# Two attention layers on one core: queries and keys contract 128 rows, the added ones zero

## The reference

```
q = einsum('oc,bcn->bon', Wq, xf) + bq[:, None]      # 32 rows
k = einsum('oc,bcn->bon', Wk, xf) + bk[:, None]      # 32 rows
v = einsum('oc,bcn->bon', Wv, xf) + bv[:, None]      # 256 rows
scores = einsum('bci,bcj->bij', q, k)
attn = softmax(scores, axis=1)
out = gamma * einsum('bcn,bnm->bcm', v, attn) + xf
```

```
energy = einsum('nid,ndj->nij', theta, phi)
attention = softmax(energy, axis=-1)
out = einsum('ncj,nij->nci', g, attention)
return gamma * conv1x1(out, out_w, out_b) + x
```

## Time and profile before

| | us |
|---|---|
| median of 3 runs | 2783.41 |
| lowest and highest | 2781.85, 2785.19 |
| the profiled execution | 2780.86 |
| its span, first to last instruction | 2779.1 |

### The profile page before, as it was taken

The page is one execution under the profiler, slowest core; times in us unless marked ns, Lnnn a source line. Parts: engine busy times, 40 slices in busy tenths (PEclk is TensorE's granted clock), DMA queues, the critical chain, the costliest instruction groups (busy, mean ns, idle before and its releaser), DMA issues.

```text
span 2779.1 us, 38409 instructions
## 1 busy us (share of the span) xinstructions
PE 2662.1 (96%) x11632; PEld 2092.5 (75%) x11632; DVE 2061.1 (74%) x3415; ACT 1743.6 (63%) x3171; POOL 1955.3 (70%) x1546
## 2 busy tenths in 40 slices
PE   7999999989999999998999999999899999999988
PEld 5777777777687777776678777777667777777756
DVE  7677777767777777776777777777676777777665
ACT  5566666667756666665765666666676566666557
POOL 3677777767867776775776776777577767777668
PEclk9999999999999999999999999999999999999989
DMA  2000000012100000001220000000121000000011
GB/s 87 1 16 16 19 21 19 21 39 69 62 31 23 16 23 16 16 16 39 70 76 24 19 21 16 16 16 16 46 77 61 16 16 16 16 16 16 16 46 62
DMA packets 45553, 85.23 MB, mean 31 GB/s; under 512 B 5032, under 2 KB 5160, under 8 KB 45352
## 3 DMA queue, kind: packets, MB, share of 16 engines
q1 hardware_dynamic: 37720, 68.41, 7.3%
q10 hardware_dynamic: 7632, 14.36, 1.7%
HBM read 48.96 MB, written 33.55 MB: 30 GB/s over the span
## 4 chain that ended last, share of the span: by engine, by line
PE 79%; DVE 11%; issue 5%; ACT 4%; POOL 1%; DMA 1%; SPq 0%; ACTq 0%; POOLq 0%; DVEq 0%
PE o_ps L908 17%; PE o_ps L911 17%; PE o_ps L912 16%; PE s_ps L885 9%; PE aux L948 8%; DVE mx L734 4%; DVE acc L696 3%; PE aux L922 2%; PE aux L986 1%; PE aux L969 1%; PE aux L965 1%; PE aux L926 1%; ACT queries L585 1%; DVE aux L775 1%; DVE osb L790 1%
## 5 line engine op out<-in xcount | busy, mean ns | idle before, releaser
L498 POOL TENSOR_TENSOR prob_l<-prob,prob_h 128x512 fp32r<-128x512 f32 x1280 | 1642.0, 1290 | 716.3 <-ACT prob_h L560 716.1
L557 ACT ACTIVATE prob<-s_ps 128x512 f32<-128x512 f32 x1280 | 766.1, 599 | 827.6 <-PE s_ps L885 824.0
L734 DVE TENSOR_REDUCE mx<-aux 128x1 f32<-128x512 f32 x1097 | 749.9, 684 | 309.1 <-PE aux L948 305.3
L908 PE MATMUL o_ps<-prob_h,vh 128*128 128x512 f32 x2304 | 926.8, 402 | 18.0 <-ACT osb L571 17.9
L911 PE MATMUL o_ps<-prob_l,vh 128*128 128x512 f32 x2304 | 914.4, 397 | 1.2 <-POOL prob_l L498 1.2
L912 PE MATMUL o_ps<-prob_h,vl 128*128 128x512 f32 x2304 | 904.7, 393 | 0.0
L696 DVE TENSOR_TENSOR acc<-prob,acc 128x512 f32<-128x512 f32 x1216 | 834.7, 686 | 76.7 <-ACT prob L557 61.8
L560 ACT ACTIVATE prob_h<-s_ps 128x512 fp32r<-128x512 f32 x1280 | 762.2, 595 | 0.0
L885 PE MATMUL s_ps<-queries,keys 98*128 98x512 f32 x1280 | 522.3, 409 | 22.7 <-DMA queries<-nm_turned 11.6
L908 PEld LDWEIGHTS o_ps<-prob_h,vh 128*128 128x128 f32 x2304 | 439.4, 191 | 129.9 <-ACT osb L571 29.2
L911 PEld LDWEIGHTS o_ps<-prob_l,vh 128*128 128x128 f32 x2304 | 438.7, 190 | 105.1 <-POOL prob_l L498 6.2
(11 more groups left out here) (131 smaller groups left out, 1886.0 us busy)
## 6 DMA issues: line engine op xcount, KB each, us to landing
xa<-x SPq DMA_DIRECT2D x32, 512.0 KB, 3.7
spill<-xa SPq DMA_DIRECT2D x32, 512.0 KB, 2.7
xa<-spill SPq DMA_DIRECT2D x32, 512.0 KB, 3.7
y<-xa SPq DMA_DIRECT2D x32, 512.0 KB, 2.8
xp<-x ACTq DMA_DIRECT2D x26, 512.0 KB, 3.7
queries<-nm_turned SPq DMA_DIRECT2D x236, 1.0 KB
xp<-x SPq DMA_DIRECT2D x2, 512.0 KB, 9.2
prob<-w_in ACTq DMA_DIRECT2D x1, 576.0 KB, 5.5
```

The lines of the kernel that those rows point to most:

```text
L498: nc.gpsimd.tensor_tensor(out=prob_l[:, i, :], in0=prob[:, i, :], in1=prob_h[:, i, :].bitcast(f32), op=ALU.subtract).then_inc(pl_ready, 1)
L557: nc.scalar.activation(prob[:, i, :], s_ps[s][:, :], ACT.Exp).then_inc(p_ready, 1)
L734: ins = nc.vector.tensor_reduce(out=dst, in_=bank[:, :], axis=AX.X, op=ALU.max)
L908: mm(o_ps[ct][:, :], value(vh, l, t, ct), prob_h[:, i, :], start=t == 0, stop=False)
```

## The change

All convolutions for keys and queries get weights of 128 columns, of which the last 32 are zero, and so write 128 rows; the bias of these rows is zero as well. ScalarE's copy of the queries to rows 64 to 95 covers rows 64 to 127 (`Q_PAD`), and so writes zeros into rows 96 to 127 of the chunk's queries; the maxima are written to rows 96 and 97 afterwards, as before. Rows 96 to 127 of `keys` are set to one at the start, in place of 96 and 97. The scores and the maxima's products contract all 128 rows: what is added is one times zero. The weights that are transferred and split are 1280 columns in place of 1152 (two parts of 640, before 576).

The order of the instructions on each engine, the waits and the plan stay as they are; only shapes change.

```
-WCOLS = 2 * R3 + C + DV
-W_KQ, W_V, W_G = (0, R3), 2 * R3, 2 * R3 + C
+WCOLS = 2 * P + C + DV
+W_KQ, W_V, W_G = (0, P), 2 * P, 2 * P + C
...
+        Q_PAD = slice(2 * DK, P)
...
-                    biased(l, q[KQ_Q, :], bank[KQ_Q, :], KQ_Q)
+                    biased(l, q[Q_PAD, :], bank[Q_PAD, :], Q_PAD)
...
-            nc.vector.memset(keys[0][NM, :].bitcast(f32), 1.0)
-            nc.vector.memset(keys[1][NM, :].bitcast(f32), 1.0)
+            nc.vector.memset(keys[0][R3:P, :].bitcast(f32), 1.0)
+            nc.vector.memset(keys[1][R3:P, :].bitcast(f32), 1.0)
...
-                mm(s_ps[h % SRING][:, :], keys[l][0:R3 + 2, t * P:(t + 1) * P], queries[0:R3 + 2, q_slot(l, b, n), :],
+                mm(s_ps[h % SRING][:, :], keys[l][:, t * P:(t + 1) * P], queries[:, q_slot(l, b, n), :],
                    start=True, stop=True).then_inc(s_full, 1)
...
-                    last = mm(dst[:, :], queries[0:R3, q_slot(l, b, c), sub * P:(sub + 1) * P],
-                              keys[l][0:R3, chunk(kc)], start=True, stop=True)
+                    last = mm(dst[:, :], queries[:, q_slot(l, b, c), sub * P:(sub + 1) * P],
+                              keys[l][:, chunk(kc)], start=True, stop=True)
...
-                    last = conv(dst[0:R3, :], W_KQ[l], R3, ROUND[Job("X", l, b, c, 0)])
+                    last = conv(dst[:, :], W_KQ[l], P, ROUND[Job("X", l, b, c, 0)])
...
+    def padded(rows):
+        return np.concatenate([rows, np.zeros((P - R3, C), np.float32)], axis=0)
-    w = np.concatenate([stacked(L0_conv_Wq, L0_conv_Wk, 0).T, stacked(L1_conv_phi_w, L1_conv_theta_w, 0).T,
+    w = np.concatenate([padded(stacked(L0_conv_Wq, L0_conv_Wk, 0)).T,
+                        padded(stacked(L1_conv_phi_w, L1_conv_theta_w, 0)).T,
                         np.asarray(L0_conv_Wv).T, np.asarray(L1_conv_g_w).T], axis=1)
```

## The result

The changed kernel takes 2745.14 us (median of 4 runs, 2742.38 to 2749.85), the kernel before 2782.63 beside it: a ratio of **0.9867, 95% interval 0.9848 to 0.9886**, 37 us less. Beside other kernels on a second occasion it took 2741.63 us against 2782.92, ratio 0.9856 (0.9841 to 0.9871). The forecast was 2737.5, 46 us less.

A forecast was written before the change was run, and what follows sets the result against it. TensorE's distances between product starts were taken to bound the kernel; -42.5 - 4 + 0.5 = -46 us took the profiled 2780.86 to 2735, and the median lying 2.5 above gave 2737.5 us, range 2724 to 2786.

The forecast's parts named there:

- What bounds the kernel: Whole span: TensorE's distance from one product's start to the next sets the time; TensorE works in 96% of the span.
- The floor and the steps: Attention steps: full products start 0.227 us apart; steps with one or two partial products fall to 1.59 and 1.82 us.
- Point 1: First layer's scores and maxima with 128 rows: 24 ns saved on each of about 1770 products, 11% left out, -42.5 us.
- Point 2: The same in the second layer: 330 products counted at half of 24 ns, -4 us, bounds 0 and -8.
- Points 3, 4 and 6: Convolutions' wider weight loads, ScalarE's wider copy of the queries with VectorE's fills, and unchanged queues: each forecast to cost nothing.
- Point 5: The start: weights of 1280 columns in place of 1152 take longer to prepare, +0.5 us, bounds 0.2 and 1.
- The clock: Around changes of layer: work that comes earlier may meet the half clock otherwise, 3 us each way.
- Rival A: Scores and maxima: their lone place between two groups costs, not their rows; no change, 2784 us; chance 0.26.
- Rival B: Scores and maxima: only the partial product's own distance shrinks, by 8 ns; 14 us less, 2770 us; chance 0.14.
- Rival C: Scores and maxima: a lone product with full rows is dearer, 5 ns more each; +9 us, 2793; chance 0.10.

## Why the prediction was right, and where it was off

- **What bounds the kernel**: right. TensorE's distances shrank and the time with them; the chain's shares are the same.
- **The floor and the steps**: right to the digit. 1.59 and 1.82 us were forecast, 1.587 and 1.813 measured. The steps with two maxima, which the forecast didn't look at, keep 13 to 18 ns of excess that has nothing to do with the row count.
- **Point 1, the size**: too large. 42.5 us over 32 chunks is 1.33 us a chunk, and 0.92 came. The step of the working that failed is the one price of 24 ns for every partial product, read from steps with one and two of them. Steps with three have 50 ns and not 72 (and 13 to 18 of the 50 are not the rows'), so the chunk held 1.2 us of excess to be won and not 1.5. And the share lost to waits, taken as 11%, was about a quarter, 0.3 of 1.2 us: beside VectorE's stretch, whose 0.19 us is what the 11% meant, there are the waits for the sums and the maxima's rows. Over the whole kernel the distances shrank by 42 us and 11 of these went into waits. That the 42 look like the forecast's 42.5 is chance: the forecast's figure is for the first layer alone and had the waits taken off.
- **Point 1, the reason**: right in its effect and wrong in its wording. Padding to 128 rows helps because everything around has 128 rows. 98 rows everywhere have the same distances.
- **Point 2, the second layer**: 4 us were forecast. From the first to the last product of attention its four stretches last 622.5 us together before, 620.7 in the first profile of the changed kernel and 613.8 in the second. The distances give 2.1 us in both, the waits take as much back (2.9 and 1.9), and what is left is the clock, 2.5 us in one and 8.3 in the other. So point 2 came to nothing, and the difference between the two profiles of one kernel is the clock.
- **Points 3, 4 and 6**, nothing: right, by the run with the padding alone. **Point 5**, half a microsecond, is too small to see; the interval of that run is 0.9988 to 1.0006.
- **The clock**, 3 us each way: too narrow, and not symmetrical. By the two levels the kernel before spends about 103 us at 1.2 GHz (a mean of 0.9815 over 2780 us), the changed one about 82 (0.985). If TensorE led in all of these 21 us, they are worth 10 us. Matched product by product the clock has 2.5 us of the gain in the first profile and 10.6 in the second, 8% and 25% of it, so it is not steady from run to run.
- **Rival A** had 0.26: out, by the runs with one odd product of attention and with 98 rows everywhere. The Trainium skill's rule that spoke for it, in "TensorE: Matmul & The Clock Gate", section "LDWEIGHTS (loading the stationary operand)", holds for the loads (189 to 191 ns for 96 to 128 rows), and says nothing of what a change of the count does to the products behind. **Rival B** is out, the whole echo went. **Rival C** is out: the distance after a full score is 0.227 us.

The errors partly cancel, and that is luck: 46 us were forecast from shorter distances net of waits, where about 31 came (42 less 11), and nothing from the clock, which gave 2.5 to 10.6.

## What to carry to other kernels

Where TensorE sets the time, read its product-to-product distances over twenty products and not the booked durations, and look for products whose number of contracted rows differs from their neighbours'. Give all of them the same number; zeros cost nothing here where rows had to be added, and one row short was as bad as thirty. An excess per item should be priced from every pattern in which the items stand, since it need not add up, and against the same pattern in the kernel after, since a part of it may have another cause. An engine that holds the chain for a while is not all that stands in the way: look at what the next one does in the same time.

## What the runs showed of the hardware that was not expected

- A change of the number of contracted rows between neighbouring products costs about 25 ns, spread over the next five products of 0.227 us. It comes both from 128 to 98 rows and back and is as large for 127 as for 98 rows. Two or three changes near one another cost 20 to 51 ns together and do not add up.
- The same row of longer distances stands behind a product that starts 5 ns late without any change of the row count, in the three-product steps of the changed kernel, where a weight load mostly starts 50 to 100 ns late. These steps are 13 to 18 ns above the floor on average.
- Changes of the bank, of the operands and of the loaded columns (96 or 128) cost nothing visible at that distance, nor do waits that are met before the weight load could start.
- The mean granted clock was lower with fewer rows in all the products: 0.976 to 0.978 with 98, 0.978 to 0.983 with 112, 0.982 to 0.987 with 128. The difference lies where TensorE has gaps, in the second layer and at the changes of layer; between the profiles with 98 rows and the two with 128 it was worth 14 and 22 us.
